# Masked copies of the gated 8-head attention: moved by pairs of heads into the steps with projections, into a second buffer

## The reference

```python
ss_g, sd_g = ss * topk_mask(ss, 3), sd * topk_mask(sd, 3)      # (b, t, 8 heads, 5 experts)
md = topk_mask(sd, 3)                                          # zeros and ones
q = einsum('bthed,bthe->bhtd', q5, sd_g)                       # k and v with ss_g
out = einsum('bhij,bhjd->bihd', softmax(q k / 8), v)
o5 = einsum('bthd,dm->bthm', out, Wo).reshape(b, t, 8, 5, 128)
x = x + tanh(g) * einsum('bthem,bthe->btm', o5, md)
```

## Time and profile before

| | |
|---|---|
| median of 3 runs | 717.81 us (716.2 to 721.22) |
| profiled execution: its time, its span | 718.16 us, 716.3 us |
| TensorE busy (matmuls), VectorE, GpSimd, ScalarE | 583.4, 507.1, 372.9, 346.6 us |
| mean granted TensorE clock | 0.885 |
| light half of the second turn | about 260 to 284.5 us of the span |

### The profile page before, as it was taken

One profiled execution on the slowest core, in us unless ns is written; L12 is line 12 of the kernel. 1 busy time (PEld: TensorE's weight loads), 2 busy tenths in 40 slices (PEclk: granted clock), 3 DMA queues, 4 the chain that ended last, 5 costly groups with the idle time before them and its releaser, 6 DMA issues. The chain is left out here.

```text
span 716.3 us, 15684 instructions
## 1 busy us (share of the span) xinstructions
PE 583.4 (81%) x5739; PEld 392.3 (55%) x5739; DVE 507.1 (71%) x1069; ACT 346.6 (48%) x750; POOL 372.9 (52%) x322
## 2 busy tenths in 40 slices
PE   5399865779859858976747879999999999878896
PEld 5277622245335425434634346677677667666785
DVE  4936899867964982895695677776767776667653
ACT  2333200042173136218542567877887886624554
POOL 5513345564744745574547456666775666632221
PEclk9999997758957985995556899999999999999998
DMA  6410000020000000000021000000000000000000
GB/s 186 110 39 31 30 30 0 0 89 1 1 1 1 0 0 0 0 0 0 30 63 56 1 1 2 2 2 2 2 3 1 3 2 2 1 2 1 2 9 26
DMA packets 14175, 13.12 MB, mean 18 GB/s; under 512 B 3120, under 2 KB 11936, under 8 KB 14112
## 3 DMA queue, kind: packets, MB, share of 16 engines
q1 hardware_dynamic: 14112, 12.25, 5.8%
HBM read 11.72 MB, written 0.52 MB: 17 GB/s over the span
## 5 line engine op out<-in xcount | busy, mean ns | idle before, releaser
L1465 POOL TENSOR_TENSOR attn<-work,attn 128x512 f16<-128x512 f32 (+1 forms) x96 | 142.0, 1481 | 85.7 <-ACT attn L1272 85.6
L808 DVE TENSOR_TENSOR work<-banks,gatev 128x512 f32<-128x512 f32 x120 | 79.3, 683 | 16.4 <-PE banks L513 15.9
L1365 DVE TENSOR_REDUCE nmax<-banks 128x2 bf16<-128x1024 f32 x64 | 77.9, 1217 | 3.0 <-PE banks L1117 1.9
L511 PE MATMUL banks<-weights,xbTh 128*128 128x512 f16 x120 | 51.2, 426 | 28.2 <-DVE work L808 26.8
L1269 ACT ACTIVATE work<-banks,maskbias 128x512 f32<-128x512 f32 x64 | 44.2, 691 | 41.5 <-PE banks L1143 41.5
L2053 PE MATMUL banks<-ident,work 128*128 128x128 f32 x276 | 52.4, 327 | 8.6 <-DVE work L2253 3.0
L943 POOL TENSOR_TENSOR work<-work 128x512 f32<-128x512 f32 x24 | 30.5, 1269 | 43.5 <-DVE work L808 41.4
L1161 PE MATMUL banks<-work,attn 128*128 128x65 f16 x512 | 51.7, 196 | 1.6 <-POOL attn L1465 1.0
L1161 PEld LDWEIGHTS banks<-work,attn 128*128 128x128 f16 x512 | 48.2, 99 | 8.0 <-POOL attn L1465 4.5
L1162 PE MATMUL banks<-work,attn 128*128 128x65 f16 x512 | 51.8, 196 | 0.0
L1163 PE MATMUL banks<-work,attn 128*128 128x65 f16 x512 | 51.7, 196 | 0.0
(11 more groups left out here) (327 smaller groups left out, 1895.0 us busy)
## 6 DMA issues: line engine op xcount, KB each, us to landing
stage<-in_L_ffn_w SPq DMA_DIRECT2D x8, 512.0 KB, 4.2
stage<-in_L_ffn_Wkv SPq DMA_DIRECT2D x4, 640.0 KB, 4.1
stage<-in_L_ffn_Wq SPq DMA_DIRECT2D x2, 640.0 KB, 5.1
xt<-in_x SPq DMA_DIRECT2D x1, 512.0 KB, 4.4
ct<-in_ctx SPq DMA_DIRECT2D x1, 512.0 KB, 5.6
wo<-in_L_xattn_Wo SPq DMA_DIRECT2D x1, 512.0 KB
stage<-in_L_xattn_Wv SPq DMA_DIRECT2D x1, 512.0 KB, 3.7
stage<-in_L_xattn_Wq SPq DMA_DIRECT2D x1, 512.0 KB, 3.5
```

Source lines behind the costliest of these rows:

```text
L511: pe.matmul(o, xh, wh, start=True, stop=False)
L808: dve.tensor_tensor(heads8(m.prod[:, k, e, :]), heads8(bank_pj[c % 2][:, :]), wide(g, DH1), ALU.mult).then_inc(s.prod_ready, 1)
L1365: dve.tensor_reduce(m.nmax[:, p % 2, i, :], banks[:, 6:8, :], AX.X, ALU.max, negate=True).then_inc(s.c_max_done, 1)
L1465: pool.tensor_tensor(m.Pl[:, p % 2, kts, :], m.Pf[:, kts, :], m.Ph[:, p % 2, kts, :], ALU.subtract).then_inc(s.c_P_lo, 1)
```

## The change

ScalarE's masked copies are made pair of heads by pair of heads: behind steps 6, 8 and 10 of the heavy half those of pairs 0, 1 and 2 (2 rows x 2 experts x 2 heads = 8 copies each), behind step 0 of the light half those of pair 3. They go into a buffer of their own, m.zm, over words of "work0" beside m.ho, of which the last batch uses a part for m.hoh and m.hol; so the wait for m.prod goes, and the wait for m.ho is for the pair alone. GpSimd's sums of a row read m.prod (3 experts) and m.zm (2 experts) in two instructions each, six in all; the wait in the chain stands behind the second of each pair.

```diff
-        m.xnT, m.cT, m.vx, m.ho, m.hoh, m.hol, m.aoT, m.xdT = share("work0", 3 * NT * P + NT * NH0,
+        m.xnT, m.cT, m.vx, m.ho, m.hoh, m.hol, m.zm, m.aoT, m.xdT = share("work0", 3 * NT * P + NT * NH0,
...
-              (0, (I, HD1), F32), (I * HD1, (I, HD1), F16), (I * HD1 * 3 // 2, (I, HD1), F16), (0, (I, HP2, P), F32),
+              (0, (I, HD1), F32), (I * HD1, (I, HD1), F16), (I * HD1 * 3 // 2, (I, HD1), F16), (I * HD1, (I, 2, HD1), F32), (0, (I, HP2, P), F32),
...
-        ACT_E, MASK_PIECE = 2, 12
+        ACT_E = 2
...
-            def masked(b, piece):
-
-                todo = [(i, e, h) for i in range(I) for e in range(E1 - ACT_E, E1) for h in range(H1)]
-                for n, (i, e, h) in enumerate(todo):
-                    if n // MASK_PIECE != piece:
-                        continue
-                    if n % (ACT_E * H1) == 0:
-                        act.wait_ge(s.O_free, b * O1 + (O1 + RING))
-                        act.wait_ge(s.prod_free, SUMS + b * GROUPS + (SUMS + i - 1))
-                    r = slice(DH1 * h, DH1 * h + DH1)
-                    at = G1 + h * E1 + e
-                    ins = act.activation(m.prod[:, i, e, r], m.ho[:, i, r], ACT.Copy, scale=m.topm[:, b * I + i, at:at + 1])
-                    if n % (ACT_E * H1) == ACT_E * H1 - 1:
+            def masked(b, o):
+
+                act.wait_ge(s.O_free, b * O1 + (o + 1 + RING))
+                for i in range(I):
+                    for e in range(E1 - ACT_E, E1):
+                        for h in (2 * o, 2 * o + 1):
+                            r = slice(DH1 * h, DH1 * h + DH1)
+                            at = G1 + h * E1 + e
+                            ins = act.activation(m.zm[:, i, e - (E1 - ACT_E), r], m.ho[:, i, r], ACT.Copy, scale=m.topm[:, b * I + i, at:at + 1])
+                    if o == O1 - 1:
                         ins.then_inc(s.z_masked, 1)
...
                 for h in range(HEAD_STEPS, STEPS):
                     step(b, h, True)
+                    if h > HEAD_STEPS and h % 2 == 0:
+                        masked(b, h // 2 - 3)
                 for h in range(HEAD_STEPS):
                     step(b + 1, h, False)
                     if h == 0:
                         high_v(b + 1)
-                    if h < 3:
-                        masked(b, h)
+                    if h == 0:
+                        masked(b, O1 - 1)
...
-                    t = m.prod[:, i, :, :].rearrange("p e (h c) -> p e h c", h=H1)
-                    ch.link(pool.tensor_tensor(t[:, :, 0:4, :], t[:, :, 0:4, :], t[:, :, 4:8, :], ALU.add))
-                    ch.link(pool.tensor_tensor(t[:, :, 0:2, :], t[:, :, 0:2, :], t[:, :, 2:4, :], ALU.add))
-                    pool.tensor_tensor(m.z[:, i, :].rearrange("p (e c) -> p e c", e=E1), t[:, :, 0, :], t[:, :, 1, :], ALU.add).then_inc(s.z_sum, 1)
+                    E0 = E1 - ACT_E
+                    t, u = (a.rearrange("p e (h c) -> p e h c", h=H1) for a in (m.prod[:, i, 0:E0, :], m.zm[:, i, :, :]))
+                    z = m.z[:, i, :].rearrange("p (e c) -> p e c", e=E1)
+                    for n in (4, 2):
+                        pool.tensor_tensor(t[:, :, 0:n, :], t[:, :, 0:n, :], t[:, :, n:2 * n, :], ALU.add)
+                        ch.link(pool.tensor_tensor(u[:, :, 0:n, :], u[:, :, 0:n, :], u[:, :, n:2 * n, :], ALU.add))
+                    pool.tensor_tensor(z[:, 0:E0, :], t[:, :, 0, :], t[:, :, 1, :], ALU.add)
+                    pool.tensor_tensor(z[:, E0:E1, :], u[:, :, 0, :], u[:, :, 1, :], ALU.add).then_inc(s.z_sum, 1)
```

## The result

| | before | after |
|---|---|---|
| median of 4 runs each | 719.28 us (716.2 to 721.22) | 711.19 us (707.31 to 712.0) |
| profiled execution: time, span | 718.16, 716.3 us | 711.09, 709.3 us |
| first exponential of a light half to GpSimd's last sum, turns 1, 2, 3 | 17.72, 17.69, 17.70 us | 15.40, 15.40, 15.39 us |

The ratio is 0.988, 95% interval 0.984 to 0.991; timed again later, 0.988 (0.982 to 0.993). The forecast was 712.4 us in a range of 707.5 to 717.0, "within 1%" the likeliest class. The measured median lies in the range; the gain, 1.2% (0.9 to 1.6%), is larger than forecast and mostly beyond that class.

A forecast was written before the change was run, and what follows sets the result against it. No engine bounds throughout; in the loop of three turns (heavy half, light half), GpSimd's and TensorE's chains tie at the light half's end. Gaining 3 x 1.8 = 5.4 us gave 712.8 on the profile's scale, median 712.4, range 707.5 to 717.0.

The forecast's parts named there:

- Two chains that tie: Light half's end: GpSimd's sums and TensorE's matmuls reach 281.31 within about 0.3 us, so neither alone is shortened with profit.
- Part 1: ScalarE's light half: 24 of 32 copies leave, so TensorE's chain gains 2.55 us per turn from the scores of head 4.
- Part 2: GpSimd's first sum in the light half: starts at 266.30 unheld or 266.89 held by VectorE's split_v, instead of 269.88.
- Part 3: GpSimd's sums in the light half: six adds per row instead of three cost 0.58 us more, 1.16 per turn.
- The sum: Whole loop: GpSimd decides, each light half ends 1.8 us earlier, 3 x 1.8 = 5.4 us, median after 712.4.
- Part 4: ScalarE's heavy half: three pieces of 8 copies, 2.0 us each, cost nothing, hidden by VectorE's products.
- The rival that made it slower: Heavy half: ScalarE's pieces come later than 1.6 us of cover allows and delay VectorE and TensorE: 730 us, chance 5%.
- Both rivals that rested on it: Light half's tail and heavy half's opening: unheld start plus better TensorE clock, 707.9, 27%; tail at half speed, 714.0, 14%.

The follow-up runs named there:

- the two one-sided runs: Changed kernel with 24 unread extra ScalarE copies in the light half: 0.9996; with the last pair's 8 copies behind step 2 instead of step 0: 1.003, both against before.
- the kernel with all copies ahead: Changed kernel with the last pair's 8 masked copies and the copies of v's upper half also ahead of the light half: 0.993 against before, 714.21 us.
- the run made to test it: Changed kernel with two unread 512-column matmuls per turn in TensorE's waits at the light half's end: 0.988 against before.
- the kernel with shared sums: Kernel with all copies ahead of the light half, GpSimd waiting for both rows' copies and summing row 0, VectorE summing row 1: 0.986 against before.

## Why the prediction was right or wrong

**Two chains that tie.** Right in the main, and shown by the two one-sided runs (0.9996 and 1.003): neither chain alone gains. In the exact order the prediction was wrong: before the change TensorE's own matmuls set the turn of the second z, and GpSimd was done 0.3 us before it. With GpSimd 2.3 us earlier the turn stayed where it was (17.98 us after the first exponential, 17.99 before). After the change it is the other way round in two turns of three, where TensorE waits 1.77 and 1.71 us for GpSimd.

**Part 1, TensorE's chain.** The scores of head 4 were to come 2.55 us earlier; they came 9.66 - 7.06 = 2.60 us earlier.

**Part 2, GpSimd's start.** The unheld start was to be 266.30 - 263.32 = 2.98 us after the first exponential; it is 2.97. That VectorE's split_v would hold it was right, shown by the run with split_v ahead: 1.80 instead of 2.27 us. The size was put at 0.59 and is 0.46.

The Trainium skill, page "SBUF — State Buffer", section "SBUF: two separate sides", says that the one that comes second blocks fully until the other's instruction ends; the 1.72 and 4.98 us of the kernel with all copies ahead agree, and the 0.46 us is 0.13 short of the 0.59 that a full block was put at. Its limit to two SBUF inputs agrees too: VectorE's L839, which has one input in PSUM, took 0.69 us at most beside GpSimd's adds.

**Part 3, the six adds: the term that was mis-sized.** The widths cost what the line through two sizes gave (5.84 us for six, worked out 5.87). But the row takes 5.85 us where it took 5.45 before, 0.40 more and not 0.58, as the second add of a pair starts some 0.05 us before the end of the first, three times per row. Row 0 without the hold shows 0.44. Together 0.84 us per turn instead of 1.16.

**The sum.** GpSimd ends 2.30 us earlier per turn instead of 1.83: 0.32 us from the adds and 0.13 from the hold. The sum was taken from GpSimd's old end, 281.01, and not from the turn of z at 281.31 that TensorE held; that adds some 0.2 us. So the turn of z comes 2.53 us earlier in each turn, 7.6 us in three and not 5.4; this is what the forecast missed by reading. The forecast time lies nearer to the measured one, 1.2 us, than the forecast gain to the measured gain, 2.7 us, by luck: the kernel before came out at 719.28 us beside it, 1.5 above the 717.81 that the forecast started from.

**Part 4, the heavy half.** Right: 29.62 and 29.58 us, L839 never waiting there. The rival that made it slower had its point at 1.6 us of cover. In the first turn the copy was pushed by 0.64 us (0.7 worked out) and the subtraction did not move; in the second it was not even pushed, as TensorE delivered it later. Its chance of 5% was not too low.

**The clock.** Both rivals that rested on it are seen within one profile: the tail at half clock in turn 2 (1.94 instead of 1.13 us) and the better clock in turns 1 and 3. I had them as alternatives, and they mix: which turn gets which changes from one execution to the next. Against the 2.53 us at the turn of z, tail and opening behind it give back 1.3 and 0.9 us in the first two turns, and the third turn gains 1.2 more. That the clock is the cause of these is read from the windows; the run made to test it did not settle it.

**What stays open.** The medians differ by 8.1 us (interval about 6 to 11), the pair of profiles by 7.1, of which the three turns hold 6.6; 1.0 us of shift is there before their loop begins, where nothing was changed, and some 0.7 us are lost again behind it. So above 7.6 us nothing is accounted for, and no more is claimed.

## What to carry to other kernels

When two chains end a stage together, price an edit on both; an edit that shortens one is worth nothing, and the same edit can be worth its full length once the other gives way, as the two one-sided runs show. Price the stage from the step that both chains feed, and not from the end of one of them. Moving work to an idle stretch of its own engine is free only where it does not bring two other engines together: start GpSimd where VectorE has no operation with two SBUF inputs, and if need be add a wait to keep them apart (0.982 against 0.986, the intervals overlapping). Before work is moved on one engine, list what stands behind it in the queues of the others; the run with both turns of z together lost 1.3% where two such copies came late.

## What was not expected

- A wait added to GpSimd made the kernel with shared sums faster, 0.986 to 0.982 (the intervals overlap); its split_v went from 3.58 to 1.28 us.
- Two engines that hold each other up at SBUF take turns, instruction by instruction: with three VectorE operations of 0.68 us beside GpSimd's adds, VectorE's took 4.98 us in all instead of 1.88, and GpSimd's row of sums 7.9 instead of 5.85.
- The last part of a light half, from GpSimd's end to the add of x, took 2.51 or 3.69 us in the changed kernel with the same instructions, depending on the turn and the execution.
- TensorE's earlier rise to the higher clock in two of the changed kernel's light halves gained nothing up to the turn of z, as TensorE then waited 1.7 us for GpSimd.
